# A two-layer window-attention kernel: normalisation for the MLP, first loads and GpSimd's powers moved between steps

## What is computed

```
x = x + norm(sigmoid(r) * wkv(k, v)) @ W_o.T        # r, k, v from mixes of layernorm(x) and its shift
y = layernorm(x)
for l in 0, 1:                                      # 8 heads of 64, windows of 128 keys and the 128 before
    q, k, v = shift(y) @ wqkv[l]
    q, k = rotary(l2norm(q) * qs), rotary(l2norm(k) * ks)
    y = y + softmax(8 * q @ k.T + mask) @ v @ wo[l]
    h = layernorm(shift(y)) * lg[l] + lb[l]
    a, g = split(h @ w1[l] + b1[l])                 # 682 each
    y = y + (a * gelu(g)) @ w2[l] + b2[l]
x = x + y
```

## Time and profile before

| | us |
|---|---|
| median of 3 runs | 2929.16 (2927.34 to 2930.24) |
| the profiled execution | 2932.18 |
| its span in the profile | 2929.9 |
| mean granted clock of TensorE | 0.984 |

### The profile page before, as it was taken

How to read it: one execution, slowest core, us unless ns; L and a number is a source line. 1 busy time by engine, 2 the same in 40 slices (tenths; PEclk the granted TensorE clock), 3 DMA queues, 4 the chain that set the end, 5 groups by cost and what they waited for, 6 DMA issues and landing times.

```text
span 2929.9 us, 67398 instructions
## 1 busy us (share of the span) xinstructions
PE 2801.9 (96%) x23076; PEld 2536.0 (87%) x23076; DVE 2202.0 (75%) x6587; ACT 2325.5 (79%) x5429; POOL 1571.2 (54%) x1524
## 2 busy tenths in 40 slices
PE   7999938899999999999999999999999999999998
PEld 6878826788998998899999899999999999999988
DVE  3979966887777778777777677777777777777773
ACT  4989946788888888888888788888888888888884
POOL 2313215656656665665566555555655655566553
PEclk9999968999999999999999999999999999999999
DMA  3252111111111111111111213111111111111111
GB/s 98 63 181 77 39 58 42 56 55 45 55 51 48 52 55 55 50 50 52 53 47 52 80 57 100 48 49 48 48 48 46 49 47 43 49 45 46 49 44 36
DMA packets 211302, 166.22 MB, mean 57 GB/s; under 512 B 21522, under 2 KB 206612, under 8 KB 209940
## 3 DMA queue, kind: packets, MB, share of 16 engines
q1 hardware_dynamic: 139284, 127.82, 14.3%
q10 hardware_dynamic: 71680, 34.10, 4.0%
HBM read 110.89 MB, written 42.58 MB: 52 GB/s over the span
## 4 chain that ended last, share of the span: by engine, by line
PE 64%; DVE 17%; POOL 6%; issue 6%; ACT 4%; DMA 1%; SPq 1%; DVEq 0%; ACTq 0%; POOLq 0%
PE ps L387 33%; PE ps L361 10%; PE ps L471 6%; PE ps L457 6%; DVE Sm L1072 5%; PE ps L445 5%; POOL rs L1218 3%; PE ps L430 2%; DVE Ar L1045 2%; POOL uTl L1304 1%; POOL r L1218 1%; DVE Gl L1145 1%; DVE Br L1046 1%; DVE Br L1047 1%; DVE oTl L1096 1%
## 5 line engine op out<-in xcount | busy, mean ns | idle before, releaser
L730 ACT ACTIVATE Sm<-Sm,nb,sc 128x256 f32<-128x256 f32 (+1 forms) x1024 | 597.4, 586 | 1.3 <-DVE nb L1079 0.5
L1072 DVE CUSTOM_DVE_ANT_0 Sm<-ps,mask 128x256 f32<-128x256 f32 (+1 forms) x1024 | 368.1, 414 | 79.6 <-PE ps L445 77.6
L387 PE MATMUL ps<-zTh,W1h 128*128 128x256 f32 (+1 forms) x1408 | 405.6, 288 | 0.0
L1145 DVE SCALAR_TENSOR_TENSOR Gl<-ps,vecs,Gl 128x256 f32<-128x256 f32 (+1 forms) x384 | 172.0, 475 | 304.2 <-PE ps L387 162.8
L387 PE MATMUL ps<-zTl,W1h 128*128 128x256 f32 (+1 forms) x1408 | 397.9, 283 | 0.0
L387 PE MATMUL ps<-zTh,W1l 128*128 128x256 f32 (+1 forms) x1408 | 393.4, 279 | 0.0
L1218 POOL TENSOR_TENSOR rs<-rs,mhalf 128x16 f32<-128x16 f32 x128 | 372.3, 2909 | 0.0
L710 ACT ACTIVATE sq<-ps 128x512 f32<-128x512 f32 x256 | 151.7, 593 | 261.7 <-PE ps L387 258.2
L1304 POOL TENSOR_TENSOR uTl<-Gl,uTh 128x512 fp32r<-128x512 f32 (+1 forms) x192 | 211.2, 1106 | 251.4 <-ACT uTh L798 199.1
L387 PE MATMUL ps<-WQh,hTh 128*128 128x512 f32 x768 | 341.5, 445 | 3.1 <-DVE hTl L1029 3.1
L387 PE MATMUL ps<-WQl,hTh 128*128 128x512 f32 x768 | 305.8, 398 | 0.0
(11 more groups left out here) (187 smaller groups left out, 8796.3 us busy)
## 6 DMA issues: line engine op xcount, KB each, us to landing
oF<-ro_scratch ACTq DMA_DIRECT2D x256, 128.0 KB, 3.0
tb<-tab SPq DMA_DIRECT2D x128, 128.0 KB, 2.3
xc<-x SPq DMA_DIRECT2D x32, 256.0 KB, 3.0
rwkv_scratch<-rw SPq DMA_DIRECT2D x32, 256.0 KB, 2.5
rk<-rwkv_scratch SPq DMA_DIRECT2D x64, 128.0 KB, 2.3
xin<-x SPq DMA_DIRECT2D x64, 128.0 KB, 2.2
x_scratch<-x SPq DMA_DIRECT2D x64, 128.0 KB, 1.7
y_scratch<-os SPq DMA_DIRECT2D x64, 128.0 KB, 4.0
```

Of the source, the lines that this page charges most:

```text
L387: ins = pe.matmul(dst, L(a), R(b), start=start and i == 0, stop=stop and i == 2)
L730: act.activation(Sm[:, h, c0:c1_], Sm[:, h, c0:c1_], ACT.Exp, bias=nb[:, h:h + 1], scale=sc[:, n % 4, h:h + 1], accum_out=sm[:, n % 2, h:h ...
L1072: dve.tensor_tensor_reduce(Sm[:, h, c0:c1_], PS[:, bank["scores", n, q, h % 2], (h // 2 % 2) * 256 + c0:(h // 2 % 2) * 256 + c1_], mask[:, ...
L1145: dve.scalar_tensor_tensor(out=Gl[0:v, j % 4, :], in0=s, scalar=V("b1a", 6 * l + j, 0, v), in1=gl, op0=ALU.add, op1=ALU.mult).then_inc(S[" ...
```

## The change

It does five things, in the second part and its beginning:

1. `z_norm` moves into the step of its statistics (t-8), behind the masked maxima; `zT`, MLP and `w2` come one step sooner (t-9, t-10, t-12 and t-11), so that the MLP stands in odd steps, and `STEPS2` falls by one. The reloads of `W1` and `W2` for the second layer move along.
2. `pre_y` moves from the head of VectorE's step to behind `z_norm`.
3. `masked_max` takes `sc` (now negative) as the scale of its fused operation and the minimum of the result, which is the bias `nb` itself. The product of line 1079 and the tile `mx` go.
4. `scale` moves into the step of the sums, behind `rot`; its power is taken in two halves, K's first.
5. The loads of `mask`, `qsks`, the first `rk` and `xin` are issued in the last steps of the first part, with tiles of their own; ScalarE waits for the group statistics instead of for `end`.

The loops over t are written out for even and odd t, and `psum_order2` follows TensorE's new order. Of the diff, the loops of VectorE (odd t) and GpSimd (odd t) and the functions:

```diff
-STEPS2 = U + 13
+STEPS2 = U + 12
...
-            w.wait_ge(S["end"], 3)
+            w.wait_ge(S["g2"], 10)
...
             def exp(n, q):
-                w.wait_ge(S["nb"], 2 * n + q + 1)
+                w.wait_ge(S["mx"], 8 * n + 4 * q + 4)
...
                     act.activation(Sm[:, h, c0:c1_], Sm[:, h, c0:c1_], ACT.Exp, bias=nb[:, h:h + 1],
-                                   scale=sc[:, n % 4, h:h + 1], accum_out=sm[:, n % 2, h:h + 1]).then_inc(S["ex"], 1)
+                                   scale=-1.0, accum_out=sm[:, n % 2, h:h + 1]).then_inc(S["ex"], 1)
...
             def masked_max(n, q):
                 c0, c1_ = cols(n)
                 w.wait_ge(S["ld2"], 32)
+                w.wait_ge(S["sc"], n + 1)
+                w.wait_ge(S["ex"], 8 * (n - 1) + 4 * q + 4)
...
-                        mask[:, n % 2, c0:c1_], 1.0, -3.0e38, ALU.add, ALU.max, mx[:, h:h + 1]).then_inc(S["mx"], 1)
-                r = slice(4 * q, 4 * q + 4)
-                w.wait_ge(S["mx"], 8 * n + 4 * q + 4)
-                w.wait_ge(S["sc"], n + 1)
-                w.wait_ge(S["ex"], 8 * (n - 1) + 4 * q + 4)
-                dve.scalar_tensor_tensor(out=nb[:, r], in0=mx[:, r], scalar=-1.0, in1=sc[:, n % 4, r], op0=ALU.mult,
-                                         op1=ALU.mult).then_inc(S["nb"], 1)
+                        mask[:, n % 2, c0:c1_], sc[:, n % 4, h:h + 1], 3.0e38, ALU.add, ALU.min,
+                        nb[:, h:h + 1]).then_inc(S["mx"], 1)
...
+                else:
+                    if live(8):
+                        z_stats(t - 8)
+                    if live(6):
+                        o_norm(t - 6)
+                    if live(7):
+                        x2_out(t - 7)
+                        zero_h2(t - 7)
+                    if live(5):
+                        o_sums(t - 5)
+                    if live(10):
+                        glu((t - 10) // 2, 0)
+                        glu((t - 10) // 2, 1)
+                        glu((t - 10) // 2, 2)
+                    if live(4):
+                        masked_max(t - 4, 0)
+                        masked_max(t - 4, 1)
+                    if live(8):
+                        z_norm(t - 8)
+                    if live(1) and t - 1 < NG:
+                        pre_y(t - 1)
+                    if live(10):
+                        u_tail((t - 10) // 2)
+                    if live(6):
+                        oT_lo(t - 6)
+                    if live(2):
+                        rope(t - 2, 1)
...
             def scale(n):
                 w.wait_ge(S["rsm"], n + 1)
-                inv_sqrt(rs[:, n % 2, :]).then_inc(S["rs"], 1)
+                inv_sqrt(rs[:, n % 2, 8:16]).then_inc(S["rs"], 1)
                 A = Ar[:, 512:1024].rearrange("p (h d) -> p h d", h=8)
                 w.wait_ge(S["kr"], n + 1)
-                w.wait_ge(S["rs"], n + 1)
+                w.wait_ge(S["rs"], 2 * n + 1)
                 pool.tensor_tensor(A, A, rs[:, n % 2, 8:16].unsqueeze(2).broadcast_to([128, 8, 64]),
                                    ALU.mult).then_inc(S["kn"], 1)
+                inv_sqrt(rs[:, n % 2, 0:8]).then_inc(S["rs"], 1)
+                w.wait_ge(S["rs"], 2 * n + 2)
                 w.wait_ge(S["ex"], 8 * (n - 4) + 8)
-                pool.tensor_scalar(sc[:, n % 4, :], rs[:, n % 2, 0:8], 8.0, None, ALU.mult).then_inc(S["sc"], 1)
+                pool.tensor_scalar(sc[:, n % 4, :], rs[:, n % 2, 0:8], -8.0, None, ALU.mult).then_inc(S["sc"], 1)
...
+                else:
+                    if live(8):
+                        root1(t - 8)
+                    if live(10):
+                        u_lo((t - 10) // 2, 0)
+                        u_lo((t - 10) // 2, 1)
+                        u_lo((t - 10) // 2, 2)
+                    if live(0) and t < NG:
+                        nT_lo(t)
+                    if live(2):
+                        rot(t - 2)
+                        scale(t - 2)
+                    if live(1):
+                        table(t - 1)
+                    if live(9):
+                        zT_lo(t - 9)
+                    if live(0) and t < NG:
+                        root0(t)
...
+                if t - 4 == NCH - 1:
+                    sp.dma_start(mask[:, :, :], mask_d).then_inc(S["ld2"], 16)
+                    sp.dma_start(qsks[:, :, :], qsk).then_inc(S["ld2"], 16)
+                    load_rk(0)
+                    load_x(0)
                 if 0 <= t - 4 < NCH:
                     store_rw(t - 4)
```

More of the change, by code:

```diff
@@ L198, in build @@
         gsh = sb("gsh", [NB, 2])
+        mask = sb("mask", [2, 256])
+        qsks = sb("qsks", [2, 256])
+        xin = sb("xin", [2, 256])
+        rk = sb("rk", [2, 2, 128])
+        nF = sb("nF", [2, 128])
+        nT = pair("nT", [2, 128])
+        tb = sb("tb", [2, 256])
+        rt = sb("rt", [2, 256])
         def V(name, i, lo=0, hi=128):
@@ L848, in scalar_program @@
[L848 to L851 removed]
+                if t % 2 == 0:
+                    if live(5):
+                        exp(t - 5, 1)
+                    if live(9):
+                        z_out(t - 9)
+                    if live(5):
+                        p_out(t - 5, 0)
+                        p_out(t - 5, 1)
+                        p_out(t - 5, 2)
+                        p_out(t - 5, 3)
+                    if live(6):
+                        oT_hi(t - 6)
+                    if live(2):
+                        square(t - 2, 1)
+                    if live(0) and t < NG:
+                        pre_norm(t)
+                    if live(5):
+                        rT_out(t - 5)
+                    if live(3):
+                        qk_hi(t - 3, 1)
+                    if live(2):
+                        square(t - 2, 0)
+                    if live(5):
+                        store_r(t - 5)
+                    if live(3):
+                        qk_hi(t - 3, 0)
+                    if live(2):
+                        v_out(t - 2)
+                    if live(4):
+                        exp(t - 4, 0)
+                    if live(5):
+                        load_r(t - 5)
+                    if live(1):
+                        hT_hi(t - 1)
+                else:
+                    if live(5):
+                        exp(t - 5, 1)
+                    if live(10):
+                        gelu((t - 10) // 2, 0)
+                    if live(5):
+                        p_out(t - 5, 0)
+                        p_out(t - 5, 1)
+                    if live(10):
+                        u_hi((t - 10) // 2, 0)
+                        gelu((t - 10) // 2, 1)
+                    if live(5):
+                        p_out(t - 5, 2)
+                        p_out(t - 5, 3)
+                    if live(10):
+                        u_hi((t - 10) // 2, 1)
+                        gelu((t - 10) // 2, 2)
+                    if live(6):
+                        oT_hi(t - 6)
+                    if live(2):
+                        square(t - 2, 1)
+                    if live(10):
+                        u_hi((t - 10) // 2, 2)
+                    if live(0) and t < NG:
+                        pre_norm(t)
+                    if live(5):
+                        rT_out(t - 5)
+                    if live(3):
+                        qk_hi(t - 3, 1)
+                    if live(2):
+                        square(t - 2, 0)
+                    if live(5):
+                        store_r(t - 5)
+                    if live(3):
+                        qk_hi(t - 3, 0)
+                    if live(2):
+                        v_out(t - 2)
+                    if live(4):
+                        exp(t - 4, 0)
+                    if live(5):
+                        load_r(t - 5)
+                    if live(1):
+                        hT_hi(t - 1)
+                    if live(9):
+                        z_out(t - 9)
@@ L1492, in sync_program @@
                     shift(t - 7)
-                if live(12) and not odd:
-                    store_out(t - 13)
+                if live(11) and odd:
                     store_out(t - 12)
-                if t - 12 == NG - 1:
+                    store_out(t - 11)
+                if t - 11 == NG - 1:
                     w.wait_ge(S["p12"], NG)
```

472 lines of the change are left out of this document (235 added, 237 removed).

## The result

The changed kernel takes **2942.2 us** (median of 5, 2941.8 to 2944.8), beside 2929.2 for the kernel before on the same chip: a ratio of 1.0046, 95% interval 1.0031 to 1.006. I had said 2902 and faster; it is slower. The profiled execution has a span of 2940.2 us against 2929.9.

What follows compares the result with a forecast made beforehand. TensorE, 96% busy, was taken to bound the kernel, so only its idle time could be gained: 5.9 + 14 + 6 + 1 = 27 us, from 2932.2 to 2905 profiled, 2902 as median; range 2882 to 2919.

Steps and rivals of the forecast that it cites:

- The passage: First part to second: ScalarE's first normalisation starts at about 411.9 instead of 417.80, 5.9 us gained; bounds 4.4 and 6.
- The filling: 437 to 581 us: K's powers come earlier and TensorE's waits for K and the residual sum go, 14 us; bounds 8, 22.
- The MLP steps of the first layer: VectorE comes 0.3 us earlier, shortening TensorE's waits for the rotary bank: 6 us gained, bounds 0 and 11.
- The GELU: First-layer MLP steps: ScalarE's third GELU no longer waits behind GpSimd's 16-column power, -1.2 us a step.
- Products and operand: First-layer MLP steps on VectorE: two products go, -0.4 us; eight maxima with scale from memory, +0.5 us.
- z and y: First-layer MLP steps: normalisation and y move from the head of VectorE's step to behind the maxima, +0.84 us.
- The second layer: No gain or loss, as TensorE is full, unless VectorE came later by more than its slack.
- The drain: End of the kernel: MLP one step sooner, last output projections behind VectorE's GLU and tail; 1 us gained, bounds -2 and 3.
- (a): VectorE gives back what GpSimd gains, in MLP steps and filling; 5.9 + 8 us remain, 2915 us; chance 0.15.
- (b): Slower: the masked maximum with scale from memory is much dearer than 0.06 us; 2958 us at 0.2; chance 0.07.
- (c): TensorE's busy rows hide waits, so the earlier GELU gains 25 us more in the second layer, 2877 us; chance 0.04.
- (d): The step saved takes 18.6 us off the end beside the other 26, 2884 us; chance 0.05.

Runs made afterwards that it cites:

- b_early: Kernel before with only the early loads and ScalarE's wait on the constants: 2923.3 us, ratio 0.9979.
- b_max: Kernel before with only the masked maximum's edit (scale from memory in the maximum, products dropped, exponential's scale constant): 2928.7 us, ratio 0.9999.
- old_max: Changed kernel with the masked maximum, its products and the exponential as before: 2947.9 us, ratio 1.006 to the kernel before.
- gap_old_max: gap with the masked maximum, its products and the exponential as in the kernel before: 2901.9 us.
- b_three: b_scale_y plus the early loads and the masked maximum's edit, so all of the change but z and the sooner MLP: 2906.7 us, ratio 0.9924.
- b_scale_y: Kernel before with GpSimd's power edit, and y before the third GLU in MLP steps, behind the maxima in others: 2908.6 us, ratio 0.9932.
- ulo: Changed kernel with GpSimd's third low part of the GLU moved behind K's rotary sum: 2913.1 us, ratio 0.9941 to the kernel before.
- gap: Changed kernel with z and y moved, in MLP steps only, between VectorE's second and third GLU: 2901.5 us, ratio 0.9901 to the kernel before.

## Why the prediction was wrong

**The passage: right.** Timeline of the changed kernel:

```profile
410.55 0.23 DVE L1081 TENSOR_TENSOR gsh<-vecs,gtm 128x2 f32<-128x2 f32 x2
410.81 0.88 ACT L753 ACTIVATE nF<-rk,gsh,gsc 128x128 f32<-128x128 f32 x2 [14.84 <-DVE gsh L1081]
...
413.19 0.55 PE L420 MATMUL ps<-Wph,nTh 128*128 128x256 f32 x1 [4.43 <-POOL nTl L1434]
```

ScalarE now waits for the constants, and 5.9 us less long than in the earlier trace rows (14.84 against 20.75), which is what I had. It starts 7.0 us sooner, and the matmul 6.9, because the constants were ready 1.07 us sooner in this execution (410.78 against 411.85). b_early, the same edit alone, gave 6.2 at n = 1 and 6.0 in the median.

**The filling: 14 forecast, 14.5 came, in part by luck.** Part of it had another source. The exponential, with its scale a constant now, takes 494 ns where it took 586; I had priced only VectorE's side of that edit. Four pairs of kernels differ by it, and from n = 0 to n = 9 it is worth 2.9 us (b_max, where the waits for `Sm` fall from 7.2 to 4.9), 3.3 (old_max), 3.4 (gap_old_max) and 0.7 (b_three beside b_scale_y), each from one execution; in the median b_max gives nothing that the runs tell. The powers with `y` moved give 9.9 us there (b_scale_y), where I had 14 for the whole. So up to 3 of the 14.5 us are the exponential's, 10 are the powers', and the rest is not placed. Groups of the kernel before (the first) and of the changed kernel, beside the earlier trace rows:

```profile
L730 ACT ACTIVATE Sm<-Sm,nb,sc 128x256 f32<-128x256 f32 (+1 forms) x1024 | 597.4, 586 | 1.3 <-DVE nb L1079 0.5
...
L794 ACT ACTIVATE Sm<-Sm,nb 128x256 f32<-128x256 f32 (+1 forms) x1024 | 502.7, 494 | 0.7
L1170 DVE CUSTOM_DVE_ANT_0 Sm<-ps,mask,sc 128x256 f32<-128x256 f32 (+1 forms) x1024 | 420.6, 476 | 95.2 <-PE ps L478 82.3
L1340 POOL TENSOR_TENSOR rs<-rs,mhalf 128x8 f32<-128x8 f32 x256 | 421.6, 1647 | 14.1
```

The maximum's operand is 0.06 us (476 against 419 ns) and the power of 8 columns 1.65 us: both priced right, from the neighbouring rows. The exponential is 92 ns shorter (586 to 494), which I had not priced. The Trainium skill (ScalarE: Activation LUTs, What ACT_TABLE_LOAD costs) says that an operand per partition adds about 93 ns to such an instruction; these rows agree.

**The MLP steps of the first layer: this is the step that failed.** I wrote "VectorE comes 0.3 us earlier". It comes 0.90 us later: from the start of the scores to K's first rotary read it was 6.33 us and is 7.23. Term by term:

- The GELU: -1.2 forecast. It starts 0.95 us sooner and the maxima 0.82, since the third GELU next waits for TensorE. I had not asked what is late next.
- Products and operand: +0.1 forecast; from the first maximum to what follows the last it was 3.32 us and is 3.24, so -0.08. Near enough.
- z and y: +0.84 forecast, from a place where GpSimd ran nothing beside them. +1.37 measured: from start to start the half of z beside GpSimd's low part takes 0.68 and the other 0.25, so 0.43 is lengthening, and 0.1 lies in the spacing of the rest.
- `oTl`: not in my sum. +0.43, since VectorE's lateness turns round who starts first against `nTl`.

The sum is -0.82 - 0.08 + 1.37 + 0.43 = +0.90. Forecast: 6 us gained. Measured: 21.8 lost from n = 10, 11 to n = 62, 63, which is what the waits say too (32.9 - 10.9 = 22.0).

How the collision comes about: GpSimd's low part waits for ScalarE, and starts 4.31 us behind the start of the scores in the trace before (787.81) and 4.30 in the changed kernel (793.81). The maxima came 0.82 us sooner and it did not, so it no longer falls on the last maxima, which keep their 0.42 us beside it, but on what stands behind them.

The rule that I weighed speaks for this. The Trainium skill (GPSIMD Engine Reference, Specifications) names two kinds of VectorE's instructions that contend with GpSimd: those with two inputs in SBUF, the on-chip memory that tiles stand in, and those in a mode that uses both ports. I quoted the first kind alone, looked at the scaled K at the end of the step, and kept the lengthening "on an engine with slack". The Trainium skill (VectorE: DVE Perf Modes, Mode 2×_2P — use both read ports for one tensor) says that a tensor-scalar operation on fp32 in SBUF gets its double rate by using both read ports, so z and y are of the second kind. The traces agree: 128 columns more cost them 0.07 us (0.34 to 0.41), where 256 more cost the two-input operations 0.27 (0.42 to 0.69); beside GpSimd 0.34 becomes 0.75 and 0.41 becomes 0.82, and ulo undoes it.

The trace before had it too, without the rule:

```profile
1914.48 0.74 POOL L1304 TENSOR_TENSOR uTl<-Gl,uTh 128x256 fp32r<-128x256 f32 x1 [3.80 <-ACT uTh L798]
1914.74 0.76 DVE L1151 TENSOR_TENSOR uTh<-Gl,uTh 42x256 fp32r<-42x256 f32 x1
...
2877.59 0.76 DVE L1130 TENSOR_SCALAR z<-x,mv,r 128x128 f32<-128x128 f32 x1
```

In the second layer GpSimd's last low part already ran beside `u_tail`, where z and y were to go, and `u_tail` took 0.76 us in the median of 29 MLP steps instead of its 0.42. And beside the very row of 1.10 us that I quoted (2877.15) z took 0.76 instead of 0.34: I read that row as GpSimd's loss and did not look at VectorE.

**The second layer: "Nothing: TensorE is full" was wrong.** It named its own condition, that VectorE's slack isn't used up, and did not work the slack out. A full TensorE says that no wait is there, not how near one is. The stretch before was 5.76 us and the limit is at 5.9: the slack was 0.1 us. It grew by 0.5 us, and 32 waits of 0.37 us came, 11.8 of the 14.5 us that the second layer lost.

**The drain: 1 forecast, 6.7 came,** outside my bounds; by b_three against gap the sooner MLP is worth about 7. In return its first step costs 3.7 us at the end of the filling, which I had not counted.

**The rivals.** (a) had the mechanism, VectorE giving back what GpSimd gains, but stopped at a gain of nothing in these steps: its price was the sum of bounds that didn't hold contention. (b) had the sign, but by another cause, which old_max and b_max refute. (c) is refuted: once the GELU came sooner without harm, in b_scale_y, the second layer ran as before (n = 72 and n = 127 are both 23.9 us ahead of the kernel before). The weight loads are busy 1003.68 of 1100 us in gap, and no kernel tried took less time than the kernel before from n = 66 to n = 126 (1112.25 us) by more than 0.1 us. The Trainium skill (Trainium Kernel Development and Optimization, Best Practices) judges the headroom by the weight loads; by these runs the other engines' waits could not use the 9% that they leave. (d) is refuted with it: a step fewer took nothing from the steady steps.

**Chances.** I gave 0.05 to slower. The term that decided, where an operation goes in VectorE's queue and what runs beside it there, had bounds of 0 and 11 us gained. An honest lower bound was z, y and `oTl` at twice their length, which goes far below zero, over the MLP steps of both layers and not of one.

**Open.** Where some 4 of the early loads' 6 us go in b_three, some 3 us of the second layer's loss beyond the waits, and 1 to 4 us of the filling.

## What to carry to other kernels

Before an operation moves on an in-order queue, take two numbers from the trace: the slack of each read behind it that frees a bank (how long from the previous engine's hand-over to the read, against how long it may take), and what the engine that shares its memory runs at the new place, once the earlier work has shifted too. Take the moved operation's duration from beside such a neighbour, not from where it stood. And look for idle time in front of it on the same queue: here the 2.1 us before the third GLU took both operations for nothing in the steady steps, and turned 13 us lost into 29 gained.

## What the runs showed of the hardware

- VectorE and GpSimd lengthen each other's fp32 instructions in SBUF, and the one that starts second pays: z 0.34 to 0.75 us beside 0.74 us of GpSimd, 0.34 to 1.31 beside 1.32, `oTl` 0.69 to 1.12; with VectorE ahead by 0.04 us it is GpSimd's `nTl` that takes 1.25 instead of 0.74, and `oTl` keeps its 0.69.
- A scale from memory instead of a constant costs 92 ns on ScalarE (586 against 494) and 57 ns on VectorE's custom maximum (476 against 419).
- GpSimd's power: 564 to 577 ns for 1 column, 1004 for 4, 1647 for 8, 2909 for 16, some 155 ns a column over a base of 0.4 us.
